# One-hot slot rows of an edge sort, made by VectorE's paired 16-bit comparison in place of ScalarE's two activations

## What is computed

```python
def _L0_gnn_ref(x, edge_row, edge_col, edge_val, W, b):
    msgs = edge_val[:, None] * x[edge_col]
    agg = jax.ops.segment_sum(msgs, edge_row, num_segments=N_NODES)
    return jnp.einsum('nf,of->no', agg, W) + b
...
xn = _layernorm(x, axis=-1)
x = x + _L0_gnn_ref(xn, src, dst, edge_weight, L0_gnn_W, L0_gnn_b) + _L0_mix_ref(xn[None], ...)[0]
x = x + _L0_ffn_ref(_layernorm(x, axis=-1)[None], ...)[0]
```

## Time and profile before

| | before |
|---|---|
| time, median of 3 runs (lowest to highest) | 1250.79 us (1250.07 to 1251.7) |
| profiled execution: span | 1249.4 us |
| PE, DVE, ACT, POOL busy | 1089.0, 800.6, 675.8, 610.4 us |
| mean granted TensorE clock | 0.946 |
| main loop, first to last matmul of the groups | 119.9 to 782.2 us |

### The profile page before, as it was taken

The page is one execution under the profiler, slowest core; times in us unless marked ns, Lnnn a source line. Parts: engine busy times, 40 slices in busy tenths (PEclk is TensorE's granted clock), DMA queues, the critical chain, the costliest instruction groups (busy, mean ns, idle before and its releaser), DMA issues.

```text
span 1249.4 us, 21035 instructions
## 1 busy us (share of the span) xinstructions
PE 1089.0 (87%) x6272; PEld 933.1 (75%) x6272; DVE 800.6 (64%) x1896; ACT 675.8 (54%) x1630; POOL 610.4 (49%) x625
## 2 busy tenths in 40 slices
PE   6797789999999999989999998716999999999990
PEld 5675677777777777767777787306999999999980
DVE  7875678888888888888888877673222222222226
ACT  4568697898978979789797874311011011011000
POOL 5937556575675766757557570002333333333320
PEclk9898899999999999999999999767999999999995
DMA  7214222232222322223223230325999999999958
GB/s 221 87 35 123 68 72 81 72 93 77 85 85 72 93 74 84 89 71 92 76 81 89 75 102 7 103 95 176 335 325 334 331 335 330 330 334 333 335 170 307
DMA packets 113487, 196.08 MB, mean 157 GB/s; under 512 B 13506, under 2 KB 61440, under 8 KB 113408
## 3 DMA queue, kind: packets, MB, share of 16 engines
q1 hardware_dynamic: 84073, 120.62, 28.8%
q0 software_dynamic: 26112, 71.34, 18.2%
q10 hardware_dynamic: 3222, 3.20, 0.7%
HBM read 177.12 MB, written 17.99 MB: 156 GB/s over the span
## 4 chain that ended last, share of the span: by engine, by line
PE 48%; DVE 14%; ACT 14%; issue 6%; DVEq 6%; POOL 6%; DMA 3%; ACTq 3%; SPq 0%; POOLq 0%
PE psum L1058 19%; PE psum L1068 9%; PE psum L964 7%; ACT in_slot L413 6%; POOL arena L702 5%; PE psum L973 3%; DVE agg L1319 2%; ACT first_use L427 2%; PE psum L895 2%; DMA arena<-y_rows,gather_i 2%; DVE agg L1325 2%; PE psum L885 2%; DVE agg L1700 1%; ACTq L414 1%; ACT arena L530 1%
## 5 line engine op out<-in xcount | busy, mean ns | idle before, releaser
L702 POOL DMA_INDIRECT arena<-y_rows,gather_i x416 | 437.5, 1052 | 250.9 <-PE psum L964 78.2
L964 PE MATMUL psum<-arena,hot 128*128 128x256 f32 x832 | 218.3, 393 | 14.9 <-issue 6.5
L635 ACT ACTIVATE arena<-psum 128x512 f32<-128x512 f32 x64 | 38.2, 597 | 327.6 <-PE psum L1058 327.6
L1319 DVE TENSOR_TENSOR agg<-psum,agg 128x256 f32 x416 | 174.6, 420 | 55.1 <-DVE agg L1319 31.0
L964 PEld LDWEIGHTS psum<-arena,hot 128*128 128x128 f32 x832 | 151.3, 192 | 49.7 <-issue 26.8
L1058 PEld LDWEIGHTS psum<-arena 128*128 128x128 f32 x1536 | 181.2, 194 | 4.9 <-issue 2.5
L530 ACT ACTIVATE arena<-arena,listed 128x256 f32<-128x256 f32 x416 | 172.6, 495 | 21.7 <-DMA arena<-y_rows,gather_i 21.7
L1058 PE MATMUL psum<-arena 128*128 128x128 f32 x1536 | 181.7, 277 | 2.0 <-DVE arena L1657 2.0
L973 PE MATMUL psum<-arena,first_use 128*128 x624 | 161.0, 394 | 25.2 <-ACT first_use L429 24.8
L1664 DVE TENSOR_TENSOR arena<-psum,arena 128x512 f32<-128x512 f32 x64 | 44.2, 691 | 204.8 <-PE psum L1058 204.8
L718 POOL DMA_INDIRECT chosen_rows<-arena,back_at x64 | 63.3, 988 | 219.7 <-DVE arena L1671 215.0
(11 more groups left out here) (227 smaller groups left out, 1634.7 us busy)
## 6 DMA issues: line engine op xcount, KB each, us to landing
arena<-in_L_ffn_w_dram SPq DMA_DIRECT2D x144, 512.0 KB, 5.8
xnT<-in_L_ffn_w_dram SPq DMA_DIRECT2D x48, 512.0 KB
arena<-y_rows,gather_i POOLq DMA_INDIRECT x416, 2.8
arena<-chosen_rows SPq DMA_DIRECT2D x4, 1280.0 KB, 9.9
y_rows<-w ACTq DMA_DIRECT2D x6, 512.0 KB, 2.9
agg<-in_x_dram SPq DMA_DIRECT2D x4, 640.0 KB, 6.6
n_rows<-arena SPq DMA_DIRECT2D x4, 640.0 KB
out_dram<-agg SPq DMA_DIRECT2D x4, 640.0 KB
```

What stands on the lines that cost most here:

```text
L702: pool.indirect_dma_start(rows[h][:, t, :], None, y_rows, bass.IndirectOffsetOnAxis(ap=gather_i[h][:, t:t + 1], axis=0)).then_inc(gathered ...
L964: pe.matmul(bank_of(g, t // 2)[:, (t % 2) * C:(t % 2 + 1) * C], hot[:, (g * GT + t) % HOTS, :], rows[h][:, t, :], start=True, stop=True).t ...
L1319: dve.tensor_tensor(own, bank_of(g, t // 2)[:, (t % 2) * C:(t % 2 + 1) * C], own, ALU.add).then_inc(evicted, 1)
```

## The change

`slot_hot` is taken from ACT, and with it the copy `place_f` of the slots with their sign turned. DVE gets `mark_slots`: one comparison for a chunk, whose output, 128 partitions x 1024 elements in bf16, is laid out in pairs of edge columns, as `in_tile` is. The slots come from `place_b`, which now holds tile and slot (64 elements in place of 32), and are compared with a constant `slot_no`, which POOL writes once at the start. PE reads `in_slot` with a stride of two elements.

```diff
-        in_slot = [sb(f"in_slot{k}", [P, CH, P], BF16) for k in range(2)]
-        place_b = sb("place_b", [P, GE], BF16)
+        in_slot = [sb(f"in_slot{k}", [P, CH // 2, P, 2], BF16) for k in range(2)]
+        slot_no = sb("slot_no", [P, P, 2], BF16)
+        place_b = sb("place_b", [P, 2, GE], BF16)
...
-            def slot_hot(g, k):
-                act.wait_ge(places_ready, g + 1)
-                if g * CHUNKS + k >= 2:
-                    act.wait_ge(reordered, g * CHUNKS + k - 1)
-                for c in range(CH):
-                    act.activation(in_slot[k % 2][:, c, :], iota[:, :], ACT.Abs, bias=place_f[:, k * CH + c:k * CH + c + 1])
-                act.drain()
-                act.activation(in_slot[k % 2][:, :, :], in_slot[k % 2][:, :, :], ACT.Relu, scale=-1.0, bias=1.0).then_inc(slot_hot_ready, 1)
...
+            pool.iota(slot_no[:, :, :], [[1, P], [0, 2]], base=0, channel_multiplier=0, allow_small_or_imprecise_dtypes=True)
...
-                    last = pe.matmul(in_order, in_slot[k % 2][:, c, :], record[k % 2][:, c // 2, :, :, c % 2].rearrange("p f t -> p (f t)"),
+                    last = pe.matmul(in_order, in_slot[k % 2][:, c // 2, :, c % 2], record[k % 2][:, c // 2, :, :, c % 2].rearrange("p f t -> p (f t)"),
...
-                dve.tensor_copy(place_b[:, :], place_i[:, 1, :])
-                dve.tensor_scalar(place_f[:, :], place_i[:, 2, :], -1.0, None, ALU.mult).then_inc(places_ready, 1)
+                dve.tensor_copy(place_b[:, :, :], place_i[:, 1:3, :])
...
+            def mark_slots(g, k):
+                if g * CHUNKS + k >= 2:
+                    dve.wait_ge(reordered, g * CHUNKS + k - 1)
+                whole = [P, CH // 2, P, 2]
+                two = place_b[:, 1, k * CH:(k + 1) * CH].rearrange("p (a b) -> p a b", b=2)
+                dve.tensor_tensor(in_slot[k % 2][:, :, :, :], two.unsqueeze(2).to_broadcast(whole), slot_no[:, :, :].unsqueeze(1).to_broadcast(whole),
+                                  ALU.is_equal).then_inc(slot_hot_ready, 1)
...
             def make_records(g, k):
                 mark_tiles(g, k)
+                mark_slots(g, k)
                 make_record(g, k)
```

More of the change, by code:

```diff
@@ L151, in gps_layer @@
         record = [sb(f"record{k}", [P, CH // 2, FIELDS, GT, 2], BF16) for k in range(2)]
-        in_slot = [sb(f"in_slot{k}", [P, CH, P], BF16) for k in range(2)]
-        place_b = sb("place_b", [P, GE], BF16)
+        in_slot = [sb(f"in_slot{k}", [P, CH // 2, P, 2], BF16) for k in range(2)]
+        slot_no = sb("slot_no", [P, P, 2], BF16)
+        place_b = sb("place_b", [P, 2, GE], BF16)
         place_i = sb("place_i", [P, 3, GE], I32)
-        place_f = sb("place_f", [P, GE])
         ends = sb("ends", [BINS, 1])
@@ L253, in gps_layer @@
         gathered = [[sem(f"gathered{h}_{q}") for q in range(GT // GC)] for h in range(2)]
-        places_ready, slot_hot_ready = sem("places_ready"), sem("slot_hot_ready")
+        slot_hot_ready = sem("slot_hot_ready")
         d_q, d_exp, d_elu, d_att, d_msg = sem("d_q"), sem("d_exp"), sem("d_elu"), sem("d_att"), sem("d_msg")
@@ L487, in _ @@
                 exp_keys(t)
-                if t in (1, 3, 5, 7):
-                    slot_hot(0, t // 2)
                 if t == 13:
                     keep_list(0)
-                if t in (19, 20, 22, 24):
-                    slot_hot(1, (19, 20, 22, 24).index(t))
             def query_exp(i):
@@ L540, in _ @@
             for g in range(NG):
-                sorts = g + 2 < NG
                 more = g + 1 < NG
@@ L571, in _ @@
                     scale_rows(g + 1, 2)
-                if sorts:
-                    slot_hot(g + 2, 0)
                 hidden_relu(g, 1)
@@ L578, in _ @@
                     act.preload_act_table(ACT.Sqrt)
-                if sorts:
-                    slot_hot(g + 2, 1)
-                    slot_hot(g + 2, 2)
                 std(1, g)
                 cross_hot(g, 2)
-                if sorts:
-                    slot_hot(g + 2, 3)
                 if more:
@@ L1167, in mark_tiles @@
                 whole = [P, CH // 2, GT, 2]
-                two = place_b[:, own].rearrange("p (a b) -> p a b", b=2)
+                two = place_b[:, 0, own].rearrange("p (a b) -> p a b", b=2)
                 dve.tensor_tensor(in_tile[:, :, :, :], two.unsqueeze(2).to_broadcast(whole), tile_of[:, :, :].unsqueeze(1).to_broadcast(whole),
@@ L1442, in beside @@
                     make_record(g + 2, 0)
+                if step == 26 and sorts:
+                    mark_slots(g + 2, 0)
                 if step == 27 and sorts:
                     mark_tiles(g + 2, 1)
+                if step == 29 and sorts:
+                    mark_slots(g + 2, 1)
                 if step == 30 and sorts:
@@ L1454, in beside @@
                     mark_tiles(g + 2, 3)
+                if step == 38 and sorts:
+                    mark_slots(g + 2, 2)
                 if step == 37:
@@ L1462, in beside @@
                     make_record(g + 2, 3)
+                if step == 44 and sorts:
+                    mark_slots(g + 2, 3)
                 if step == 43:
```

## The result

The changed kernel takes 1263.23 us (median of 4 runs, 1262.87 to 1264.24) against 1250.75 (4 runs, 1250.07 to 1251.7) for the kernel before on the same chip. The ratio is 1.0103, 95% interval 1.0089 to 1.0117. The prediction was 1263.4. The profiled execution spans 1262.5 us, 13.1 more than before.

A forecast was written before the change was run, and what follows sets the result against it. DVE was taken to bound the loop. From the execution's span, 1249.4 - 5 (prologue) + 0.6 (group 0) + 17 (groups 1 to 10) = 1262.0; the runs' median lies 1.4 above: 1263.4 us, range 1254 to 1273.

The forecast's parts named there:

- DVE bounds the loop: Loop groups 1 to 10: DVE's sequence alone takes the 51.8 us a group; PE's stop for ACT is inside PE's lead.
- What a comparison costs: Groups 1 to 10: 0.70 us long; 0.31 more each at steps 26 and 29, 0.61 each at 38 and 44.
- The prologue: Before the loop: eight one-hots leave ACT, eight comparisons join DVE; 5 us gained, bounds 2 and 8.
- Group 0: First loop group: three comparisons fall into DVE's waits for PE, the fourth shows; 0.6 us more.
- Left at zero: Groups 11 and 12, which don't sort, and the stretch after the loop: 0 us change.
- No wait of PE for L419: Loop sign: PE no longer waits for ACT's last piece of `cross_hots`, before 2.1 us a group.
- More waits for L1306: Loop sign: PE waits more for DVE's evictions at L1306 and L1312; no size given.
- ACT on the path: Rival, loop: PE's 2.1 us wait a sorting group ends, DVE's extra work fits its idle time; 1223 us, chance 0.10.
- the condition that the prediction set: ACT's rival decides if the 0.04 us touches of DVE and product at steps 49 to 55 are real waits in most groups.
- Cancelling: Rival: comparisons cost only 0.1 to 0.2 us each, loop loses about 5 us, prologue returns it; 1251 us, chance 0.05.
- One element a cycle: Rival: each comparison takes 1.21 us like `hot`, 20 us more in loop, 2 in prologue; 1285 us, chance 0.03.
- POOL: Rival, loop: DVE's added two-input work holds up POOL and gathers come late; 1268 us, chance 0.02.

The follow-up runs named there:

- dve_load: Kernel before, with the four comparisons added on DVE in loop groups 0 to 10 into an unread buffer, ACT's one-hots and `place_f` kept: 1267.64 us, ratio 1.0141.
- twice_again: Changed kernel with each loop comparison made a second time into an unread buffer, on a chip where the kernel before takes 1250.37 us: 1288.38 us, ratio 1.03.
- swap_hots_again: Changed kernel with ACT making `hot` from loop group 1 on and DVE's four `hot` comparisons a group gone: 1232.53 us, ratio 0.9859 to the kernel before.
- act_load: Changed kernel with ACT's old nine activations put back at their old places in loop groups 0 to 10, into an unread buffer: 1264.22 us, ratio 1.0107.
- prologue_only: Changed kernel with DVE's comparisons only for the two groups sorted in the prologue, ACT's activations for groups 2 to 12: 1244.73 us, ratio 0.9961.
- twice: Changed kernel with each loop comparison made twice, on the slow chip where the kernel before took 1327.63 us: 1362.0 us, ratio 1.0267.

## Why the prediction was right

**DVE bounds the loop.** Right. DVE's load alone lengthens it by 17 us (dve_load), twice the load by another 23 (twice_again), and taking `hot` off DVE shortens it by 32 (swap_hots_again); 136 us of ACT's work put back into the changed kernel change nothing (act_load).

**What a comparison costs.** The duration was forecast at 0.70 us and is 0.687 on the mean. The price by neighbour was forecast at 0.31 twice and 0.61 twice; in group 5 it is 0.31 twice, 0.58 and 0.60, and the same to 0.01 us in nearly every other of groups 1 to 10. The net was forecast at 1.7 us a group and is 1.76, and 1.71 for the comparisons alone in dve_load, both a little below the 1.84 that I had for the four. The gain of 0.15 that I took off for `place_f` does not show; two small errors of opposite sign bring the net so near, which is luck.

The Trainium skill, "VectorE: DVE Perf Modes", section "The DRAIN you can't avoid", would by its first sentences give the full duration each, 2.65 us a group, and 1273 us. The same section adds that a next operation that is not held back starts earlier, and the prediction left that out. The runs bear the addition out: even the second comparison of twice_again, with no wait to fill, costs 0.57 of its 0.68 us, and the next instruction starts 0.08 us ahead of its recorded end. What they do not bear out is that a semaphore costs nothing: an eviction behind an eviction starts 0.21 us after its end.

**The prologue.** The mechanism was right: 5 forecast, 4.4 at the first matmul and 3.5 at the first eviction, and 5.8 at the first matmul in prologue_only, whose work up to there is the same. The 1.4 us between these two kernels are older than any comparison. The first scan of the sort, before, in the changed kernel and in prologue_only:

```profile
43.87 2.19 DVE L1128 TENSOR_TENSOR_SCAN count<-in_bin 128x800 f32<-128x800 bf16 x1
45.54 2.19 DVE L1107 TENSOR_TENSOR_SCAN count<-in_bin 128x800 f32<-128x800 bf16 x1
44.14 2.19 DVE L1125 TENSOR_TENSOR_SCAN count<-in_bin 128x800 f32<-128x800 bf16 x1
```

It starts at 43.9 to 44.1 or at 45.5 to 45.6 us, and both occur with the old prologue (before, dve_load) and with the new one. What decides between them is open. From the scan to the loop's first matmul it is 76.0 and 75.1 us with ACT's one-hots (before, dve_load), 70.0 in the changed kernel and in prologue_only, and 70.3 to 71.9 in the other four kernels with DVE's. The means differ by 4.9 us: that is what moving the one-hots gave. The changed kernel's profile shows 6.1 from the scan on, less the 1.7 us by which its sort began later.

**Group 0.** Forecast +0.6, measured +0.1 from eviction to eviction. The first eviction came late, though, 2.2 us behind the first matmul in place of 1.3. From the first matmul to group 1 it is 67.4 us before, 68.4 in the changed kernel, 68.3 in prologue_only, which has no comparison there, and 68.5 in dve_load, which has them behind the old prologue. These runs don't tell what the comparisons cost in this group.

**Left at zero.** Groups 11 and 12 have grown by 0.7 and the stretch after the loop has shrunk by 1.8. Nothing of the change is in the latter; it took 466.5 us before and 463.9 to 465.2 in the seven other profiles outside the slow chip, so I take it for scatter from one profiled execution to the next. The errors against the forecast of each part are +1.5 (prologue), -0.5 (group 0), +0.6, +0.7 and -1.8, together +0.5. The total was nearer than its parts, and that is luck.

**The sign of what would show it.** "No wait of PE for L419" was wrong: 0.7 us a group are left, behind ACT's wait for DVE. "More waits for L1306" was wrong too (4.4 us, as before); those for L1312 and L1347 grew.

**The rivals.** ACT on the path: refuted for the changed kernel by act_load. For the kernel before, dve_load leaves DVE 0.13 us a group of room at most, and the condition that the prediction set can be read in the trace: the eviction of step 51, which comes 0.04 to 0.41 us behind its product in six groups, starts 0.05 to 0.08 us ahead of the end of what DVE did before it in all ten, so DVE never stood still for it. The margin was thin: by these rows a little more lateness of ACT would have reached DVE, which no run here tries. The Trainium skill ("Perfetto Trace Analysis", section "Identifying the Most-Contended Engine") goes by occupancy, but for TensorE by the busy share of its weight loads, which the prediction left out. By busy matmuls PE is named (92.6%), by weight loads (75.5%) ACT is, with 86.5% against 85.4% for DVE; the runs name DVE. PE's wait for ACT shrank by 14 us and the groups grew by 18. Cancelling: the gaps swallow 0.3 of two comparisons in four, no more. One element a cycle: 0.687 us rules it out. POOL: its busy time in the groups is 332.5 us, no more than the 337.8 of before, and no wait of the loop's engines for its gathers grew.

## What to carry to other kernels

Before work is moved off an engine that somebody waits for, set the time at which each product is ready beside the time at which its consumer takes it, at the step right behind the wait. If the consumer is still late there, the wait is inside the producer's lead, and neither shares of busy time nor lists of waits will say so. On the engine that bounds, an instruction costs the distance it adds between its neighbours' starts, so put it where a self-wait is (0.31 against 0.60 us here). Where an engine is relieved off the path, look for what it could take from the one that bounds: in the loop ACT's freed time was worth nothing until DVE's `hot` was moved into it, and the kernel then was 1.4% faster than before.

## What the runs showed of the hardware

- A bf16 comparison of 128x1024 with both inputs broadcast, laid out in pairs, takes 0.68 us, little more than half of the 1.21 us that the fp32 one of the same size takes. ACT pays the same for either: 2.43 and 1.06 us for eight Abs and a relu, in bf16 (act_load, rows below) as in fp32 (`cross_hots`, in ACT's rows of the changed kernel above). So it is the fp32 one-hots that are better moved to ACT.

```profile
422.81 2.43 ACT L413 ACTIVATE spare<-iota,epsc 128x128 bf16<-128x128 f32 x8
425.32 1.06 ACT L415 ACTIVATE spare<-spare 128x1024 bf16<-128x1024 bf16 x1
```

- Loading weights with a stride of two bf16 elements takes 97 ns, without one 96.
- One chip ran the kernel before 6% slower than the others did. In the profile of twice there DVE stands 47.2 us in ten waits (one a group) whose releaser the profile cannot place, with PE's product already made. What causes them is open.
